# Two transformer layers on one core: routing of the last expert layer moved into a rebuilt gate, its residual, norm and output into the expert stage

## What is computed

```python
x = _layernorm(x + L0_attn(x)); x = _layernorm(x + L0_ffn(x))
x = _layernorm(x + L1_attn(x)); x = _layernorm(x + L1_ffn(x))
```

```python
_stats(x) = [mean(x), var(x), mean(abs(x)), l2norm(x)]        # over the 32 channels of a head
gin = concat([hs, _stats(short), _stats(long), _stats(delta), _stats(v)])
logits = (gelu(gin @ gW1 + gb1) @ gW2 + gb2) / exp(log_temp)
probs = softmax(logits) * (1 - sum(floor)) + floor
o = sum over the 4 branches of probs[a] * branch[a]
o = o + sigmoid(conv_res) * short + alpha_id * (hs @ Wid)
o = o * rsqrt(mean(o * o) + 1e-5) * o_norm_w
return o @ Wo
```

```python
logits = xf @ gate_w + gate_b
pb = softmax(logits); idx = top_k(pb, 1)
out = pb[idx] * (gelu(xf @ w1[idx] + b1[idx]) @ w2[idx] + b2[idx])
```

## Time and profile before

| | us |
|---|---|
| median of 3 runs (lowest, highest) | 1529.68 (1529.28, 1536.52) |
| the profiled execution, its own time | 1537.19 |
| its span | 1535.0 |
| mean granted TensorE clock over the span | 0.742 |

### The profile page before, as it was taken

The page is one execution under the profiler, slowest core; times in us unless marked ns, Lnnn a source line. Parts: engine busy times, 40 slices in busy tenths (PEclk is TensorE's granted clock), DMA queues, the critical chain, the costliest instruction groups (busy, mean ns, idle before and its releaser), DMA issues. The chain is left out here.

```text
span 1535.0 us, 34540 instructions
## 1 busy us (share of the span) xinstructions
PE 1000.4 (65%) x13068; PEld 766.8 (50%) x13069; DVE 841.9 (55%) x2298; ACT 588.0 (38%) x1111; POOL 336.7 (22%) x351
## 2 busy tenths in 40 slices
PE   6776787767719999245563948855777664505950
PEld 2454555545619999123232747753456433505950
DVE  3655667756435555178775851115767774212436
ACT  1444444444405555265664221103344433103530
POOL 0111321333324444345331011000000000061025
PEclk9888888878559999577676967655665576557985
DMA  3202222122412221222322141130121110711213
GB/s 93 48 16 53 67 53 59 40 62 64 149 45 62 60 60 51 81 76 71 74 56 45 42 63 18 19 80 20 42 76 41 48 42 14 254 40 52 68 48 96
DMA packets 182433, 93.86 MB, mean 61 GB/s; under 512 B 63534, under 2 KB 173969, under 8 KB 182176
## 3 DMA queue, kind: packets, MB, share of 16 engines
q1 hardware_dynamic: 175904, 79.37, 20.5%
q0 software_dynamic: 6400, 12.67, 2.6%
HBM read 56.72 MB, written 35.79 MB: 60 GB/s over the span
## 5 line engine op out<-in xcount | busy, mean ns | idle before, releaser
L1515 ACT ACTIVATE bx_h<-bx_up,bx_cur 128x128 f32<-128x128 f32 x288 | 82.1, 368 | 101.2 <-PE bx_up L1494 101.2
L617 ACT ACTIVATE a_at<-a_scores 128x1024 f32<-128x1024 f32 x64 | 65.3, 1021 | 113.1 <-PE a_scores L468 113.1
L463 PE MATMUL a_scores<-a_rk,a_kx 32*128 32x128 f32 (+3 forms) x1024 | 64.3, 329 | 59.2 <-DVE a_at L809 56.4
L538 POOL TENSOR_TENSOR a_vx<-a_vx,a_con 128x2048 f32<-128x2048 f32 x8 | 36.2, 4522 | 286.5 <-DMA a_vx<-lion_values 286.5
L1456 POOL DMA_INDIRECT chosen_b<-bx_ys,bx_to x72 | 74.2, 1031 | 97.5 <-DVE bx_ys L1544 95.7
L463 PEld LDWEIGHTS a_scores<-a_rk,a_kx 32*128 32x128 f32 x1024 | 48.3, 222 | 85.4 <-DVE a_at L809 70.1
L1494 PE MATMUL bx_up<-bx_xT,bx_cur 128*128 128x128 f32 x576 | 81.8, 286 | 2.5 <-DVE bx_cur L1529 2.5
L1476 PE MATMUL bx_down<-bk_w,bx_h 128*128 x576 | 81.9, 286 | 0.4 <-ACT bx_h L1515 0.4
L1494 PEld LDWEIGHTS bx_up<-bx_xT,bx_cur 128*128 128x128 f32 x576 | 70.9, 194 | 9.2 <-DVE bx_cur L1529 4.2
L530 POOL DMA_INDIRECT regions_b<-a_xo,a_seat x64 | 63.6, 994 | 49.3 <-DVE a_seat L781 28.1
L1476 PEld LDWEIGHTS bx_down<-bk_w,bx_h 128*128 128x128 f32 x576 | 69.7, 191 | 2.9 <-issue 0.8
(11 more groups left out here) (397 smaller groups left out, 2650.2 us busy)
## 6 DMA issues: line engine op xcount, KB each, us to landing
a_vx<-lion_values SPq DMA_DIRECT2D x32, 256.0 KB, 5.1
bx_xs<-regions_b SPq DMA_DIRECT2D x72, 65.0 KB, 1.8
bk_w<-in_b_w SPq DMA_DIRECT2D x16, 256.0 KB, 5.8
c_part<-chosen_b SPq DMA_DIRECT2D x16, 256.0 KB, 4.0
g_X<-rows SPq DMA_DIRECT2D x16, 256.0 KB, 4.8
d_w<-in_d_w SPq DMA_DIRECT2D x16, 256.0 KB, 6.0
sorted_d<-dr_zero SPq DMA_DIRECT2D x4, 640.0 KB, 7.0
de_xs<-sorted_d SPq DMA_DIRECT2D x10, 256.0 KB, 2.7
```

The source lines that it names most:

```text
L463: mm(S4[:, g, o:o + P - 32 * q], kx[rows, 0, 4 * t + q].rearrange("p h j -> p (h j)"), rk[b][rows, 0, t * P + 32 * q:(t + 1) * P], start=T ...
L617: op(at[m % 2][:], S4[:, :, 0:320].rearrange("p g (q k) -> p g q k", q=2)[:, :, :, 0:P], ACT.Copy).then_inc(s_ata, 1)
L1515: i = op(h[u % 2][:, f, :], BU[u % 2][:, f * P:(f + 1) * P], act_fn, bias=cur[u % 2][:, FC * P + f:FC * P + f + 1])
```

## The change

`moe_stage` with its three parts is gone. `gate_stage` is written anew and contains the routing; `expert_stage` gets a variant (`norm`) that serves the last layer, also with 40 tiles. In detail:

- **Statistics from raw moments.** No centering: ACT squares the branches as they are (`square`), DVE sums values, squares and absolute values (three reductions), and two instructions of 64 elements give the variance times 32. The factors 1/32 are in the weights `g1s`. The l2 norm is the sum of squares to the power 0.5, on POOL.
- **Powers on POOL.** All square roots and reciprocals of the gate (l2 norm, deviation of the mixed rows, deviation of the sum, reciprocal of the top-1 sum) are `tensor_tensor(..., ALU.pow)` on POOL against a column of constants, and one for each tile in the last expert stage.
- **Logits with held weights.** `gw2`, widened to 32 columns, is the stationary side: four products of 128x512, one per head, each to 32 partitions. ACT scales and biases them in one instruction, and four products against a constant (`sel16`) turn them by row.
- **Mixing.** One product of 128x2048 on DVE, two pair sums on POOL, the identity branch added by DVE.
- **Sum and norm.** Residual and projected rows go to `Z`, 136 columns wide: the last 8 are the expert gate's logits, from weights that are multiplied in advance (`wox`, `idx8`). ACT writes the normed rows (scale and shift per row) to `xo`.
- **Routing.** `sum_stats`, `best`, `choose`, `dispatch`, `top_sums` on DVE, `deviations`, `pick_sums`, `scatter` on POOL, `count` on PE, Exp on ACT, one or two groups behind the mixing. POOL scatters four times per group to `regions_d`. The table of the 40 tiles comes at the end (`tile_table`, the code of the first routing as a function).
- **Loads.** The residual comes as `xT`, channel major (2 KB per partition), which `delta_project` now stores in place of the rows. The expert weights load during the gate.
- **Last expert stage.** ACT copies the expert weights (`fetch`, with its register load) ahead of the Gelus. DVE adds the bias, multiplies by the row's weight and adds the residual row, takes its statistics; POOL gives the deviation; DVE norms one tile later, POOL scatters to `out`.
- The gate becomes a stage of its own, so one more barrier of all engines stands ahead of it. The 8 groups are written out, where six of them were in a loop.

Core of the diff (the new functions by name; what is left out is of the same kind):

```diff
@@ expert_stage, POOL
+            def deviation(j, u):
+                pool.wait_ge(s_z, j + 1)
+                nc.gpsimd.tensor_scalar(vr[:, u:u + 1], mv[:, u, 1:2], LN_EPS, None, ALU.add).then_inc(s_vr, 1)
+                pool.wait_ge(s_vr, j + 1)
+                nc.gpsimd.tensor_tensor(rsv[:, u:u + 1], vr[:, u:u + 1], power[:], ALU.pow).then_inc(s_rs, 1)
...
@@ expert_stage, ACT
+            def fetch(j, u):
+
+                e = act.value_load(expert[0:1, bass.ds(j, 1)], min_val=0, max_val=NE - 1)
+                op(cur[u % 2][:], w1[:, bass.ds(e, 1), :].rearrange("p e c -> p (e c)"), ACT.Copy).then_inc(s_cur, 1)
+
             def body(g, last):
                 for u in range(U):
                     j = g * U + u
+                    if norm and (u < U - 1 or not last):
+                        after(act, s_h, j)
+                        fetch(j + 1, (u + 1) % U)
                     act.wait_ge(s_up, j + 1)
@@ expert_stage, DVE
+                if norm:
+                    dve.wait_ge(s_b, j + 1)
+                    v.scalar_tensor_tensor(z[u][:], yb[u % 2][:], xs[u][:, P + 1:P + 2], xs[u][:, 0:P], ALU.mult, ALU.add
+                                           ).then_inc(s_res, 1)
+                    dve.wait_ge(s_res, j + 1)
+                    v.bn_stats(bst[:, u, :], z[u][:]).then_inc(s_bn, 1)
+                    dve.wait_ge(s_bn, j + 1)
+                    after(dve, s_st[u], g * 16)
+                    v.tensor_copy(to[u][:], xs[u][:, P:P + 1])
+                    v.bn_aggr(mv[:, u, :], bst[:, u, :]).then_inc(s_z, 1)
+                    return
...
+            def normed(j, u):
+                dve.wait_ge(s_rs, j + 1)
+                v.tensor_scalar(ys[u][:], z[u][:], mv[:, u, 0:1], rsv[:, u:u + 1], ALU.subtract, ALU.mult).then_inc(s_y, 1)
@@ delta_project, SP and ACT
-                sp.wait_ge(s_xn, 4 * n + 4)
-                sp.dma_start(one(x_tiles, n), xn[:]).then_inc(s_xo, 16)
+                sp.wait_ge(s_xT, n + 1)
+                sp.dma_start(xT_groups[bass.ds(n, 1)].rearrange("g p t -> (g p) t"), xT[:]).then_inc(s_xo, 16)
...
-            def copy_x(m):
+            def copy_x(m, first=False):
                 act.wait_ge(s_T, m + 1)
+                if not first:
+                    act.wait_ge(s_xo, 16 * m)
@@ gate_stage, POOL
+            def mixed(n):
+                pool.wait_ge(s_mix, n + 1)
+                op.tensor_tensor(half[:], mix[:, 0:2], mix[:, 2:4], ALU.add).then_inc(s_half, 1)
+                pool.wait_ge(s_half, n + 1)
...
+                op.tensor_tensor(osum[:], half[:, 0], half[:, 1], ALU.add).then_inc(s_os, 1)
...
+            for n in range(NG):
+                if n + 1 < NG:
+                    norms(n + 1)
+                if n:
+                    deviations(n - 1)
+                mixed(n)
+                mixed_deviation(n)
+                if n:
+                    pick_sums(n - 1)
+                if n >= 2:
+                    scatter(n - 2)
+            deviations(NG - 1)
+            scatter(NG - 2)
+            pick_sums(NG - 1)
+            scatter(NG - 1)
@@ gate_stage, PE
+            def logits(m):
+                for h in range(NH):
+                    pe.wait_ge(s_hid, 4 * m + h + 1)
+                    i = mm(S[32 * h:32 * h + 32, :], gw2[:], hid[:, h, :], start=True, stop=True, skip_group_check=True)
+                i.then_inc(s_lt, 1)
+                pe.wait_ge(s_lgT, m + 1)
+                for t in range(GT):
+                    i = mm(S[:, t * NH * NA:(t + 1) * NH * NA], lgT[:, tiles[t]], C["sel16"], start=True, stop=True)
...
@@ gate_stage, DVE
+            def statistics(m):
...
+                v.tensor_reduce(st4[:, :, :, 0], X[b][:], AX_X, ALU.add).then_inc(s_s0, 1)
...
+                v.tensor_reduce(ssq[:], xc[:], AX_X, ALU.add).then_inc(s_ssq, 1)
+                v.tensor_reduce(st4[:, :, :, 2], X[b][:], AX_X, ALU.add, apply_absolute_value=True)
+                dve.wait_ge(s_s0, m + 1)
+                v.scalar_tensor_tensor(msq[:], st4[:, :, :, 0], 1.0 / 32, st4[:, :, :, 0], ALU.mult, ALU.mult).then_inc(s_msq, 1)
+                dve.wait_ge(s_msq, m + 1)
+                v.tensor_tensor(st4[:, :, :, 1], ssq[:], msq[:], ALU.subtract).then_inc(s_st, 1)
...
+                v.tensor_tensor(mix[:], X[n % 2][:], pr[:].rearrange("p j a -> p a j").unsqueeze(3).broadcast_to([P, NA, TH, 32]),
+                                ALU.mult).then_inc(s_mix, 1)
+                if n:
+                    best(n - 1)
+                dve.wait_ge(s_os, n + 1)
...
+                v.tensor_tensor(o[:], osum[:], I.rearrange("p (j c) -> p j c", c=32), ALU.add).then_inc(s_o, 1)
+                if n:
+                    choose(n - 1)
+                dve.wait_ge(s_o2, n + 1)
+                v.tensor_reduce(ms[:], o2[:], AX_X, ALU.add).then_inc(s_ms, 1)
...
+                dve.wait_ge(s_rms, n + 1)
+                v.tensor_tensor(on[:], o[:], wide(rms[:], 32), ALU.mult).then_inc(s_on, 1)
+                if n:
+                    dispatch(n - 1)
```

More of the change, by code:

```diff
@@ L871, in _ @@
-            then(v.tensor_copy(ends[:], run[0:1, :]))
-            dispatch(NG - 1, 1)
-            for q in range(3):
-                a, b, d = base[q % 2], base[1 - q % 2], 1 << q
-                then(v.tensor_tensor(b[:, 4:], a[:, 4:], a[:, 4 - d:4 + NE - d], ALU.add))
-            j_of = C["tiles"][0:1, 0:NT_TOP2]
-            then(v.tensor_tensor(le[:], base[1][:, 4:].unsqueeze(1).broadcast_to([1, NT_TOP2, NE]),
-                                 j_of.unsqueeze(2).broadcast_to([1, NT_TOP2, NE]), ALU.is_le))
@@ L1385, in expert_stage @@
-def expert_stage(nc, sem, tag, regions, dest, route, keep, NT, act_fn, consts):
+            dispatch(NG - 1, 1)
+            tile_table(v, then, run, C, cnt, over, base, skipped, le, lt, ef, ends, NT_TOP2, route).then_inc(s_tab, 1)
+def expert_stage(nc, sem, tag, regions, dest, route, keep, NT, act_fn, consts, norm):
     where, columns = constant_columns("ident", "ident")
@@ L1404, in expert_stage @@
         to = [sb(f"to{i}", [P, 1], U32) for i in range(U)]
+        z = [sb(f"z{i}", [P, P]) for i in range(U if norm else 0)]
+        bst = sb("bst", [P, U, 6])
+        mv = sb("mv", [P, U, 2])
+        vr = sb("vr", [P, U])
+        rsv = sb("rsv", [P, U])
+        power = sb("power", [P, 1])
         yb = [sb(f"yb{i}", [P, P]) for i in range(2)]
@@ new lines, in gate_stage @@
+        mine = sb("mine", [P, GT, NE])
+        pf = sb("pf", [P, GT])
+        seat = [sb(f"seat{i}", [P, GT], U32) for i in range(2)]
+        se = sb("se", [P, GT])
+        pad = sb("pad", [P, ROW])
+        cnt = sb("cnt", [1, NE])
+        over = sb("over", [1, NE, TOK // P])
+        base = [sb(f"base{i}", [1, 4 + NE]) for i in range(2)]
+        skipped = sb("skipped", [1, NE])
+        le = sb("le", [1, NT, NE])
+        lt = sb("lt", [1, NT, NE])
+        ef = sb("ef", [1, 2, NT])
+        ends = sb("ends", [1, NE], I32)
@@ new lines, in _ @@
+            sp.dma_start(route["regions"][DUMMY * P:DUMMY * P + P], pad[:]).then_inc(s_pads, 16)
+            for dst, src in route["weights"]:
+                sp.dma_start(dst, src).then_inc(s_mw, 16)
+            for n in range(NG - 2):
+                sp.wait_ge(s_mix, n + 1)
+                load_branches(n + 2)
+                if n + 3 < NG:
+                    sp.wait_ge(s_pj, n + 1)
+                    load_x(n + 3)
+            sp.wait_ge(s_tab, 1)
+            for e in range(NE):
+                end = sp.value_load(ends[0:1, e:e + 1], min_val=0, max_val=e * REGION + TOK)
+                sp.dma_start(route["regions"][bass.ds(end, P), :], pad[:]).then_inc(s_pads, 16)
@@ new lines, in top_exps, with norm @@
+            def top_exps(n):
+                act.wait_ge(s_te, n + 1)
+                op(tex[n % 2][:], te[:], ACT.Exp).then_inc(s_tex, 1)
+            def norm(n):
+                b = n % 2
+                act.wait_ge(s_nb, n + 1)
+                if n >= 2:
+                    act.wait_ge(s_scat[b], 64 * (n // 2))
+                for t in range(GT):
+                    i = op(xo[b][:, t, 0:P], zrow(t), ACT.Identity, bias=shift[b][:, t:t + 1], scale=rsv[b][:, t:t + 1])
+                i.then_inc(s_xo, 1)
@@ L2465, in step @@
+            square(0)
+            act.wait_ge(s_wg, 1)
+            op(won[:], S[:, 0:P], ACT.Copy).then_inc(s_wgc, 1)
+            act.wait_ge(s_wg, 2)
+            op(wox[:, P:ZC], S[:, P:P + NE], ACT.Copy)
+            op(gsum[:], S[:, P + NE:P + 2 * NE], ACT.Copy).then_inc(s_wgc, 1)
+            statistics(0)
+            gelu(0)
+            act.wait_ge(s_pv, 1)
+            logits(0)
+            for n in range(NG):
+                if n + 1 < NG:
                     square(n + 1)
-                    norms(n + 1)
@@ L2467, in step @@
                 act.wait_ge(s_sh, n + 1)
                 op(pr[:], lg[:], ACT.Exp).then_inc(s_ex, 1)
-                if not last:
-                    if not first:
-                        act.wait_ge(s_pj, n)
```

(9 more changed lines are left out.)

1049 lines of the change are left out of this document (378 added, 671 removed).

## The result

The changed kernel takes 1452.9 us (median of 4 runs, 1448.5 to 1457.0) against 1529.5 for the kernel before (median of 4); ratio 0.949, 95% interval 0.944 to 0.954. It is faster, as forecast, by 77 us where 137 were forecast: 1453 lies outside the range of 1370 to 1424. The profiled execution took 1456.8 us, its span is 1455.0 (1535.0 before), its mean granted clock 0.763.

The account below looks back on a forecast made before the run. Bounds: serial routing and gathering, and the gate's ring through DVE, ACT and PE. Gate periods of 25.5, its start and end, and 40 tiles of 2.3 cut the span from 1535.0 to 1398; 1529.7 - 137 = 1393 us, range 1370 to 1424.

Parts of the forecast that it names:

- first logits: Start of the gate: DVE reads the first group's logits at 1066 us instead of 1071.9.
- the seven periods: Gate: time per group of 512 tokens falls from 30.4 to 25.5 us; seven of these, less 4.5, end at 1240.
- last iteration: End of the gate: the last group's iteration runs serially, with counts and seats done after 33.5 us.
- tiles: Last expert stage: 40 tiles at 2.3 us, bound by ACT, and 2 us for the first at the slow clock.
- 0.15 us for 1 or 4 columns, 0.3 for 16, 0.6 for 64: Gate: assumed time of each POOL power by its width; no profile row showed a power.
- upper bound of 1.16: Most a POOL power was thought to take, in us: the mean of 128x128 TENSOR_SCALAR with pointer operands beside a busy DVE.
- is hidden by PE's lateness: Gate: the 64-wide power costs nothing, since PE turns the statistics only from 12.1 us on; cover from 5.1 to 12.1.
- power loop: Rival, gate: POOL's power loops over single elements, c us each; at 0.35 the time is 1573 us; chance 0.04.
- The first rival: Gate: POOL becomes the bound, its small instructions at 1.16 us; period 29.5, time 1421 us; chance 0.17.
- The walk: Gate: one iteration followed step by step through the engines from DVE's read of the logits, giving a period of 25.5 us.
- 23.7 if PE is never late: Gate: length of one iteration in us along DVE, POOL and ACT, if PE holds nothing up.
- clock rises: Rival: PE pauses less and is granted 2.4 GHz; period 23.5, quicker start and end, 1372 us; chance 0.09.

Follow-up runs that it names:

- a1: Changed kernel with POOL's 64-wide power (l2 norms) replaced by a multiplication of the same shape, so not computing in full; ratio 0.910 to the kernel before.
- b2: Changed kernel with the l2 norms by Sqrt on ACT in place of POOL's power, computing in full; median 1406.6 us, ratio 0.914 to the kernel before.
- a3: Changed kernel with all of POOL's powers in the gate replaced by multiplications, so not computing in full; ratio 0.895 to the kernel before.
- after: The changed kernel itself as first measured and profiled, against the kernel before; 1452.9 us, ratio 0.949.
- b3: b2 with the deviation of the mixed rows also by Sqrt on ACT and a reciprocal on DVE; median 1391.7 us, ratio 0.906 to the kernel before.
- a4: Changed kernel with ACT's register load ahead of its wait for its own Gelus in the last expert stage; ratio 0.938 to the kernel before.
- c1: b3 (pair sums left on POOL) with ACT's register load ahead of its wait as in a4, computing in full; median 1384.0 us, ratio 0.902 to the kernel before.

## Why the prediction was right or wrong

The time came out 60 us over the forecast's 1393, the span 57 over its 1398. By its own steps: first logits 1068.7 for 1066, +2.7; the seven periods 218.7 for 174, +44.7; last iteration 38.3 for 33.5, +4.8; table and barrier -2.1; tiles 95.8 for 94, +1.8; end 13.0 for 8.3, +4.7.

**The step that failed** is the price "0.15 us for 1 or 4 columns, 0.3 for 16, 0.6 for 64" with its upper bound of 1.16. Measured: 0.57, 1.04, 2.92 for 16, 10.61 for 64. With it fell the sentence that the 64-wide one "is hidden by PE's lateness". a1 and b2 show that this one instruction makes 45 to 53 us of the time, a3 that all powers of the gate make 80. The upper bound came from an operation of another kind: the price of a multiplication with pointers says nothing about a cost of 0.16 us per column. The rival "power loop" had the mechanism: with c = 0.16 its own formula, 8 x (84 x 0.16 - 6.9), gives 52 us, near the 60 that were missed; 0.29 was its point of no gain. Its chance of 0.04 rested on "no POOL row costs over 0.01 us per element", but no row was a power. The first rival (POOL as bound, 1421) had the right engine with the wrong reason: its small instructions cost 0.2 to 0.6, not 1.16.

**A second error lay on the other side and hid.** The walk without any power price comes to about 25 us, and a3 measured 22.1. It charged PE's four 128x512 products at the lower clock, 6.4 us as in the earlier trace rows, and so had the statistics turned at 12.1; the row after is 3.60, the identity branch takes 1.05 in a3 for the 2.07 charged, and there the statistics are turned at 7.6. What sets a3's period is then the walk's other path, "23.7 if PE is never late". The granted clock of the gate's periods was 0.66 in after and 0.78 in a3 (154.7 us), 0.61 in the earlier trace rows. The start hides the same: its +2.7 holds a 64-wide power that PE waits out in full (10.6), and in a3 first sum to first logits is 10.7 shorter, so there the forecast was some 8 us too long. The part "clock rises", at 0.09, was thus half true. With cheap powers I would have missed by 20 us to the other side: the 60 us are 80 for the powers less these 20, and that the miss was not larger is luck.

**What held.** DVE's steps: product of the mixing done 12.3 us into the iteration (13.5 said), no instruction of DVE over 2.3 us but for the contention below; the pair sums 2.33 + 1.26 (2.3 + 1.3 said); the logits' products overlapped; the last iteration 33.4 in a3, where the powers are cheap (33.5 said). ACT's table loads: 1.28 each with the next activation 0.02 behind; b2's one more per iteration moved the period by 0.2 against a1, and b3's two more did not keep it from falling to 23.6. The "five table loads per group" of the kernel before are four in its trace (34 in the 8 groups with their start), which no term of the sum used. The Trainium skill, ScalarE: Activation LUTs, section "What ACT_TABLE_LOAD costs", would add a drain of some 1.4 us to each; by these rows there is none that costs time. Last stage: 2.33 per tile (2.3 said), bound by ACT with its register load, as a4 shows; POOL's part of a tile, said to be 1.7, is 2.2 (c1). The routing held nothing up: POOL's four scatters end 4.3 us into the next iteration, before the power's input is there.

**Small misses.** The end: behind the last Gelu come DVE's result, POOL's deviation 0.25 + 0.57 and two issues in order, so the last scatter is issued 7.15 us later (4.6 said), and the program ends 5.85 behind that (3.7 said, from a row with an ordinary store).
